# Chunk 0's dense layers woven into the stream that builds the low-rank factors, in a conditioned recurrent kernel

## The chip, the cores and the metric

The kernel runs on one core of one Trainium2 chip. The metric is the device time of one execution in microseconds, the median of several runs.

## What is computed

The reference, cut to what matters (B = 16, T = 512, D = 512, rank 8; `erf` GELU):

```python
c = layernorm(cond) * gamma + beta                  # [16, 512]
h = gelu(c @ W1 + bias1)
w = h @ W2 + bias2                                  # W2 is [512, 16384]
a1, b1, a2, b2 = [t.reshape(B, D, 8) for t in split(w, 4)]
u = einsum('btd,bdr->btr', x, a2)
mid = gelu(x @ down + einsum('btr,blr->btl', u, b2))
v = einsum('blr,btl->btr', b1, mid)
x1 = x + x + mid @ up.T + einsum('bkr,btr->btk', a1, v)
xW = x1 @ Wx + b
h_0 = cond;  h_t = tanh(xW[:, t] + h_{t-1} @ Wh)    # 512 steps, one after the other
y = x1 + h
```

So each batch row has low-rank factors of its own, made from the conditioning vector by one large product with W2 (33.6 MB), and the result of the dense layers drives a recurrence.

## The kernel before

Numbers are split into a high and a low part (`HI`, `LO`) and multiplied in three passes (`PASSES`), so that each product of 128 rows costs three matmuls per 128 of the contraction. The split is two operations: ScalarE rounds the high part (a cast), DVE subtracts it from the number to get the low part. Recurrent weights and states are split in the same way into two 16-bit parts.

Time is cut into NC = 16 chunks of TC = 32 steps; a chunk is 512 columns (16 batches by 32 steps). The work comes in this order:

- **Prologue.** Layer norm of cond on DVE, the product with W1 on TensorE (L795), GELU on ScalarE (L442, L443), transposes of Up (L802) and its split, the split of Down (high half on ScalarE, L426, low half on POOL, L410).
- **The factor stream.** W2 is read in 32 halves of 1 MB through a ring of four buffers of `work` (`load`, L358). For each half n: `w2_high(n)` casts it on ScalarE (L434), `w2_low(n)` subtracts on DVE (L608), TensorE multiplies the high part and then the low part by h, eight matmuls (L835), ScalarE copies the row to `wrow` (L473). Each second half closes a factor tile: TensorE spreads it by eight transposes (L822), DVE sums the parts (L625) and adds the bias (L632, four adds of 64 columns), for half of the tiles TensorE turns it (L810), then ScalarE and DVE split it (L463, L639). There are two pairs of split buffers, `act_s` and `mid_s`. A ring buffer is free when `w2_low` has read it. SP issues everything in its order: the 16 pieces of chunk 0's x (L304) stand between loads, ahead of the last four halves, then Wx and Wh.
- **Chunk 0's dense work.** Slots -23 to 31 of `dense_slot(0, r)` for each engine: transpose x (L661), split it (L491, L669), the rank product U (L850), Mid = x with Down (L861) plus its rank part (L864), GELU and split (L502, L503, L690), the rank product V, Out = Mid with Up, the sum x1 (L694) and its split (L508, L699), XW = x1 with Wx, scaled into `xw` (L513). Each engine walks a list of slots written out ahead (`MID_SLOTS`, `OUT_SLOTS`, `XW_SLOTS`, `XT_AT` and the like). Chunk 0 has nothing beside it but the splits of Wx (L534, L410) and Wh (L537, L770) and the search for Wh's scale.
- **The recurrence.** Step n of chunk c: ScalarE places xW(n) in PSUM (`place`, L481), TensorE multiplies the state by Wh in four quadrants of eight matmuls (L882), DVE sums (L724), ScalarE takes tanh (L529), DVE splits the state (L729, L732), POOL adds the state to x1 (L417). Between steps TensorE does slot t of the dense work of chunk c + 1. Step 0 multiplies by Wh in float32 (L877). In the last chunk three idle matmuls a step take the place of dense work.
- **Store.** x1 plus state is transposed (L707) and stored by SP, 16 DMAs a chunk (L378).

## Time and profile before

| | us |
|---|---|
| median of 3 runs | 1348.98 (1348.88 to 1351.66) |
| the profiled execution | 1356.64 |
| its span, first to last instruction | 1354.9 |
| TensorE busy in the span | 1273.1 (94%) |
| VectorE (DVE) busy | 983.7 (73%) |
| ScalarE (ACT) busy | 702.6 (52%) |
| GpSimd (POOL) busy | 266.6 (20%) |

The profiled execution is 7.7 us above the median; 1.7 us of it lie outside the span. TensorE is busy 90% or more from the sixth of the forty slices on; the first five slices, 170 us, are where it is not. The mean granted TensorE clock is 0.972 of full speed. In the windows below, PEclk is that clock, 1.00 being 2.4 GHz and 0.50 being 1.2 GHz; PE is TensorE's matmuls, PEld its weight loads, SPq the queue that issues DMAs.

### The profile page before, as it was taken

What the parts mean: (1) busy time and instruction counts of PE and PEld (TensorE: products, weight loads), DVE (VectorE), ACT (ScalarE), POOL (GpSimd) and SP (SyncE); (2) the same over time, 40 slices, a digit from 0 to 9 for tenths busy, and PEclk for the clock granted to TensorE, in tenths of its full rate; (3) what the DMA queues carried; (4) which work ended last, traced back from release to release, by engine and by line L of the source; (5) the groups of instructions that cost most, each with busy time, mean ns of one, the idle gap of its engine ahead of it and who ended that gap; (6) DMA issues with size and microseconds to landing.
All of it is one profiled execution on the core that took longest, in us unless ns stands there. A gap on an engine that the chain in (4) does not pass through costs nothing.

```text
span 1354.9 us, 49302 instructions
## 1 busy us (share of the span) xinstructions
PE 1273.1 (94%) x20268; PEld 1019.6 (75%) x20268; DVE 983.7 (73%) x3755; ACT 702.6 (52%) x2499; POOL 266.6 (20%) x525
## 2 busy tenths in 40 slices
PE   6775789999999999999999999999999999999995
PEld 4332478888888888888888888888888888888764
DVE  5665754778787878777777778787878787877564
ACT  5554433555555555555555555555555555555442
POOL 1000010222222222222222222222222222222111
PEclk9788799999999999999999999999999999999998
DMA  8777611113121212121212212111222121202021
GB/s 289 255 246 225 189 26 16 18 18 49 18 49 18 44 24 41 26 42 25 38 30 33 34 28 35 26 31 32 34 33 34 24 43 18 34 3 34 2 34 32
DMA packets 292271, 75.63 MB, mean 56 GB/s; under 512 B 273072, under 2 KB 273088, under 8 KB 292048
## 3 DMA queue, kind: packets, MB, share of 16 engines
q1 hardware_dynamic: 292048, 72.49, 24.0%
q8 instruction: 160, 2.62, 0.9%
q14 instruction: 63, 0.52, 0.2%
HBM read 55.68 MB, written 16.78 MB: 53 GB/s over the span
## 4 chain that ended last, share of the span: by engine, by line
PE 76%; DVE 9%; ACT 7%; issue 3%; DMA 3%; SPq 1%; POOL 0%; DVEq 0%; POOLq 0%; ACTq 0%
PE bulk L861 38%; PE rec L882 28%; PE bulk L850 4%; PE bulk L864 4%; ACT hf L529 3%; DMA work<-in_L_cond_W_dram 2%; DVE act_s L608 2%; PE bulk L835 2%; DVE act_s L699 2%; DVE z L724 2%; ACT rec L481 1%; DVE mid_s L608 1%; SPq L304 1%; DVE work L694 1%; ACT act_s L508 1%
## 5 line engine op out<-in xcount | busy, mean ns | idle before, releaser
L882 PEld LDWEIGHTS rec<-hs,wh_s 128*128 128x128 f16 x16352 | 442.7, 96 | 141.2 <-DVE hs L732 138.1
L529 ACT ACTIVATE hf<-z,scl 128x32 f32<-128x32 f32 x1024 | 273.7, 315 | 499.8 <-DVE z L724 495.5
L882 PE MATMUL rec<-hs,wh_s 128*128 128x32 f16 x16352 | 493.2, 177 | 12.7 <-ACT rec L481 10.4
L417 POOL TENSOR_TENSOR work<-work,hf 128x64 f32<-128x64 f32 x512 | 255.8, 500 | 909.8 <-DVE hs L732 909.8
L724 DVE TENSOR_REDUCE z<-rec 128x32 f32<-128x96 f32 x1024 | 229.8, 255 | 123.2 <-PE rec L882 104.1
L729 DVE TENSOR_SCALAR hs<-hf 128x32 f16<-128x32 f32 x1024 | 181.7, 177 | 106.6 <-ACT hf L529 106.5
L732 DVE SCALAR_TENSOR_TENSOR hs<-hf,hs 128x32 f16<-128x32 f32 x1024 | 197.0, 192 | 35.3
L861 PE MATMUL bulk<-mid_s,up_s 128*128 128x512 f32 x768 | 219.1, 409 | 0.0
L861 PE MATMUL bulk<-act_x,down_s 128*128 128x512 f32 x768 | 218.2, 407 | 0.0
L861 PE MATMUL bulk<-act_s,wx_s 128*128 128x512 f32 x768 | 207.3, 407 | 0.0
L481 ACT ACTIVATE rec<-work 128x32 f32<-128x32 f32 x1024 | 183.9, 209 | 0.0
L861 PEld LDWEIGHTS bulk<-act_s,wx_s 128*128 128x128 f32 x768 | 135.9, 189 | 22.5
L861 PEld LDWEIGHTS bulk<-mid_s,up_s 128*128 128x128 f32 x768 | 132.7, 190 | 17.7
L861 PEld LDWEIGHTS bulk<-act_x,down_s 128*128 128x128 f32 x768 | 132.7, 190 | 17.7
L835 PE MATMUL bulk<-act_s,h_s 128*32 128x512 f32 x128 | 44.0, 480 | 33.8 <-DVE act_s L608 23.1
L513 ACT ACTIVATE work<-bulk,bs,scl 128x512 f32<-128x512 f32 x64 | 48.0, 776 | 23.6 <-PE bulk L861 23.2
L835 PEld LDWEIGHTS bulk<-act_s,h_s 128*32 128x32 f32 x128 | 13.5, 124 | 54.7 <-DVE act_s L608 31.3
L699 DVE TENSOR_TENSOR act_s<-work,act_s 128x512 fp32r<-128x512 f32 x64 | 44.2, 690 | 14.2 <-ACT act_s L508 14.2
L434 ACT CAST act_s<-work 128x2048 fp32r<-128x2048 f32 x16 | 30.5, 1904 | 42.8 <-DVE act_s L608 24.6
L835 PE MATMUL bulk<-mid_s,h_s 128*32 128x512 f32 x128 | 43.8, 485 | 8.1 <-DVE mid_s L608 8.1
L690 DVE TENSOR_TENSOR mid_s<-gel,mid_s 128x512 fp32r<-128x512 f32 x64 | 43.8, 684 | 9.2 <-ACT mid_s L503 9.2
L694 DVE SCALAR_TENSOR_TENSOR work<-work,bulk 128x512 f32<-128x512 f32 x64 | 43.6, 682 | 7.5 <-PE bulk L864 6.2
(114 smaller groups left out, 1027.3 us busy)
## 6 DMA issues: line engine op xcount, KB each, us to landing
work<-in_L_cond_W_dram SPq DMA_DIRECT2D x33, 1024.0 KB, 5.6
work<-in_x_dram SPq DMA_DIRECT2D x256, 64.0 KB, 3.5
out_dram<-work SPq DMA_DIRECT2D x256, 64.0 KB, 2.4
work<-in_L_cond_base_up_dram SPq DMA_DIRECT2D x1, 1024.0 KB, 6.1
work<-in_L_cond_base_down_dram SPq DMA_DIRECT2D x1, 1024.0 KB, 7.7
work<-in_L_cond_Wx_dram SPq DMA_DIRECT2D x1, 1024.0 KB, 4.9
work<-in_L_cond_Wh_dram SPq DMA_DIRECT2D x1, 1024.0 KB, 5.0
bias2T<-in_L_cond_bias_dram SPq DMA_DIRECT2D x4, 16.0 KB, 3.5
```

The costliest lines, as they stand in the source:

```text
L417: nc.gpsimd.tensor_tensor(xs, xs, hf[:, t % 4], ALU.add).then_inc(sum_done, 1)
L481: nc.scalar.activation(R[f][:, :, PARTS, :], xw[:, c % 2].rearrange("p k (b t) -> p k b t", t=TC)[:, f * HT:(f + 1) * HT, :, t], ACT.Copy) ...
L529: nc.scalar.activation(hf[:, t % 4, half], z[:, half], ACT.Tanh, scale=inv).then_inc(tanh_done, 1)
L694: nc.vector.scalar_tensor_tensor(out=x1[n % 3][:, m], in0=x1[n % 3][:, m], scalar=2.0, in1=bulk[:, BANK_OUT[m], :], op0=ALU.mult, op1=ALU. ...
L699: nc.vector.tensor_tensor(act_s[:, LO, m], x1[n % 3][:, m], act_s[:, HI, m].bitcast(F32), ALU.subtract).then_inc(x1lo_done, 1)
L724: nc.vector.tensor_reduce(z[:, f * HT:(f + 1) * HT], R[f].rearrange("p m j b -> p m b j"), AX.X, ALU.add).then_inc(z_done, 1)
L729: nc.vector.tensor_scalar(hs[:, half, 0, :], hf[:, t % 4, half], H_SCALE, None, ALU.mult).then_inc(hi_done, 1)
L732: nc.vector.scalar_tensor_tensor(out=hs[:, half, 1, :], in0=hf[:, t % 4, half], scalar=H_SCALE, in1=hs[:, half, 0, :], op0=ALU.mult, op1=A ...
L835: last = nc.tensor.matmul(bulk[0:2 * B, BANK_ROW + n % 2, :], h_s[:, k].rearrange("p s b -> p (s b)"), w2_s[n % 2][:, part, k, :], start=( ...
L850: last = nc.tensor.matmul(bulk[:, out_bank, g * GC:(g + 1) * GC], fac_s[:, k, g, :], src[:, a, k, g * GC:(g + 1) * GC], start=(k == g == a ...
L861: mm = nc.tensor.matmul(bulk[:, banks[m], :], w_s[:, w, k, m * P:(m + 1) * P], src[:, a, k, :], start=(i in starts), stop=(i in ends), ski ...
L882: last = nc.tensor.matmul(R[fo][:, m, 0:PARTS, :], wh_s[:, q, k, n * P:(n + 1) * P], hs[:, k, :, :], start=(m == k == q == 0), stop=(k == ...
```

## The change

Five things change.

1. Chunk 0's dense work is given a plan of its own (`FIRST`), in pieces fixed by hand: `PE_FILL`, `ACT_FILL` and `DVE_FILL` say behind which half of the stream (0 to 38) each engine does which slots of `dense_slot(0, r)`. Its items are ordered so that the rank parts come late (`first_items`), and TensorE waits once for each factor tile where a piece first needs it. Slots 24 to 31, the product with Wx, come behind the stream, with the first slots of chunk 1. x of chunk 0 is loaded four pieces at a time behind loads 5 to 8 of the ring.
2. Wh is loaded second of all, into a buffer of its own, and its maximum, its scale and its split (high half at half 0, low half at half 1 of the stream) are done ahead. Step 0's product with Wh is done in the prologue, on 16 columns (`first_state`); step 0 is then an add on DVE.
3. A third pair of split buffers, `wx_s`, up to half 17; from half 18 `act_s` and `wx_s` are the two, and `mid_s` serves the dense work. The split of a factor comes one half later on DVE; the bias is added in two operations and not four; `wrow` has memory of its own.
4. PSUM banks are dealt anew, with waits for their release. Chunks 1 to 15 keep their plan but for the slots of x1's low half and of the splits of x. The place of xW for the next step stands ahead of the dense work at a chunk's end too.
5. Small DMAs (norm vectors, bias2) are issued by ScalarE's queue, and half of the last chunk's 16 stores too. Twelve transposes are added on TensorE ahead of its first work.

The diff, cut:

```diff
-BANK_MID = (1, 2, 3, 4)
+BANK_MID = (1, 2, 3, 1)
-BANK_OUT = (5, 1, 2, 3)
-BANK_XW = (4, 5, 1, 2)
+BANK_OUT = (2, 3, 1, 2)
+BANK_XW = (4, 5, 1, 3)
+WARM_MM = 12
+def first_items(kt):
+    items = [(m, k, p) for m in range(kt - 1) for k in range(kt) for p in range(len(PASSES))]
+    items += [(m, g, -1 - w) for m in range(kt - 1) for g in range(GROUPS) for w in (HI, LO)]
+    items += [(kt - 1, k, p) for k in range(kt) for p in range(len(PASSES))]
+    return items + [(kt - 1, g, -1 - w) for g in range(GROUPS) for w in (HI, LO)]
+STREAM = 39
+PE_FILL = {6: (0,), 7: (1,), 8: (2,), 9: (3,), 10: (4,), 11: (5,), 13: (-2,), 21: (6,), 22: (7,), 23: (8,), 27: (12,),
+           28: (13,), 29: (10,), 30: (14,), 31: (15,), 32: (16,), 33: (17, 18), 34: (19,), 35: (20, 21), 36: (22,),
+           37: (23,)}
+ACT_FILL = {3: (-20, -16), 4: (-7, -6), 14: (-2,), 22: (6,), 23: (7,), 24: (8,), 30: (10,), 35: (19,), 36: (20,),
+            37: (21,)}
+DVE_FILL = {2: (-21, -17), 3: (-8, -7), 4: (-6, -5), 5: (-4, -3), 14: (-1,), 15: (0,), 16: (1,), 23: (7,), 25: (8,),
+            26: (9,), 31: (11,), 32: (12,), 33: (13,), 34: (18,), 35: (19,), 36: (20,), 37: (21,), 38: (23,)}
+FIRST_TAIL = 24
+WH_HI_AT, WH_LO_AT, WX_HI_AT = 0, 1, 35
...
-        w2_s = (act_s, mid_s)
+        w2_s = [(act_s, mid_s, wx_s)[n % 3] if n < 18 else (act_s, wx_s)[n % 2] for n in range(HALVES)]
...
+        FIRST = {"u": (-2,) * KT, "v": (10,) * KT,
+                 "mid": stage_plan(first_items(KT), cuts(0, (6, 12, 18, 24, 30, 36, 44, 54, 64))),
+                 "out": stage_plan(first_items(KT), cuts(12, (6, 12, 18, 24, 30, 36, 40, 44, 48, 54, 60, 64))),
+                 "xw": plan(False, FIRST_TAIL, (1,) * 8), "x1lo": (19, 20, 21, FIRST_TAIL)}
...
         def _(sp):
             sp.dma_start(cn[:, 0, :], cond).then_inc(cond_in, 16)
+            sp.dma_start(wh_f, wh.rearrange("(k p) n -> p k n", p=P)).then_inc(wh_in, 16)
             sp.dma_start(w1_f, w1.rearrange("(k p) n -> p k n", p=P)).then_inc(w1_in, 16)
...
+            for e in range(WX_ENTRY + 1):
                 load(e)
+                if e == RING + 1:
+                    sp.wait_ge(hT_mm, 1)
+                if RING < e <= RING + KT:
+                    load_x(0, e - RING - 1)
...
+            store_y(NC - 1, (0, 1))
+            sp.wait_ge(y_out, IN_OUT * NC)
...
         def _(act):
+            for i in range(STREAM):
+                if i + 2 < HALVES:
+                    w2_high(i + 2)
+                if i % 2 and 0 <= i // 2 - 2 <= LAST:
+                    factor_high(i // 2 - 2)
+                if i < HALVES:
+                    row_copy(i)
+                for r in ACT_FILL.get(i, ()):
+                    dense_slot(0, r)
+                if i == WH_HI_AT:
+                    act.wait_ge(scl_done, 1)
+                    nc.scalar.activation(wh_s[:, 0], wh_f, ACT.Identity, scale=w_scale).then_inc(wh_hi, 1)
+                if i == WX_HI_AT:
+                    arrived(act, WX_ENTRY)
+                    nc.scalar.copy(wx_s[:, HI], wx_f).then_inc(w_hi, 1)
...
         def _(dve):
+            for i in range(STREAM):
+                if i < HALVES:
+                    w2_low(i)
+                if i % 2 == 0 and 0 <= i // 2 - 3 <= LAST:
+                    split_factor(i // 2 - 3)
+                if i % 2 == 0 and 0 <= i // 2 - 2 <= LAST:
+                    factor(i // 2 - 2)
...
+                for r in DVE_FILL.get(i, ()):
+                    dense_slot(0, r)
...
         def _(pe):
+            pe.wait_ge(wh_in, 16)
+            pe.wait_ge(h0T_done, 1)
+            first_state(0)
+            first_state(1)
+            pe.wait_ge(ln_chain, 10)
             for k in range(KT):
+                last = nc.tensor.transpose(bulk[:, 0, k * B:(k + 1) * B], cn[:, 1, k * P:(k + 1) * P], ident[0:B, 0:B])
             last.then_inc(cond_tr, 1)
+            first_state(2)
+            first_state(3).then_inc(h0_mm, 1)
...
+                for i in mid[1].get(r, ()):
+                    m, k, p = mid[0][i]
+                    if i in mid[2] and m in (0, 2):
+                        need(pe, xw_done, (n - 1) * KT + 3 + m // 2)
+                    if i in mid[2] and m == KT - 1:
+                        pe.wait_ge(gel_done, n * KT + 1)
+                    if n == 0 and p == -1 and k == 0:
+                        pe.wait_ge(fac_split, KT + m + 1)
...
+            for i in range(STREAM):
+                if i < HALVES:
+                    row(i)
+                if i % 2 and 0 <= i // 2 - 1 <= LAST:
+                    spread(i // 2 - 1)
+                if i % 2 == 0 and 0 <= i // 2 - 2 <= LAST and W2_TILES[i // 2 - 2][0] in (0, 3):
+                    turn(i // 2 - 2)
+                for r in PE_FILL.get(i, ()):
+                    dense_slot(0, r)
```

## Rows read from the trace of the kernel before

**Rows 1.** Timeline of DVE in the stream: start us, us, engine, line, operation, tiles

```profile
28.37 2.29 DVE L608 TENSOR_TENSOR act_s<-work,act_s 128x2048 fp32r<-128x2048 f32 x1 [0.87 <-ACT act_s L434]
...
153.75 2.28 DVE L608 TENSOR_TENSOR act_s<-work,act_s 128x2048 fp32r<-128x2048 f32 x1
...
155.95 0.42 DVE L625 TENSOR_REDUCE fsum<-rec 128x128 f32<-128x256 f32 x1
...
156.40 0.77 DVE L632 TENSOR_TENSOR fac<-fsum,bias2T 128x64 f32<-128x64 f32 x4
157.09 2.28 DVE L608 TENSOR_TENSOR mid_s<-work,mid_s 128x2048 fp32r<-128x2048 f32 x1
```

**Rows 2.** The chain of waits, 186 to 228 us: start us, us, what

```profile
186.62 5.47 PE bulk L861 x24
...
207.19 12.27 PE bulk L861 x48
219.46 1.93 PE bulk L850 x16
...
227.24 0.81 PE rec L882 x32
```

**Rows 3.** Windows by stage: stretch, its length, then each engine's busy us

```profile
core 0: us, PE busy (x) PEld busy (x) DVE busy (x) ACT busy (x) POOL busy (x), PEclk, DMA share, GB/s
26.00:38.00 12.00, 11.36 (x47) 5.12 (x45) 10.32 (x12) 9.51 (x8) 0.00 (x0) 1.00 0.98 353
38.00:50.00 12.00, 6.63 (x24) 2.83 (x23) 6.15 (x9) 7.15 (x7) 0.00 (x0) 0.70 0.71 245
48.00:110.00 62.00, 47.55 (x184) 21.61 (x182) 43.82 (x62) 37.39 (x37) 0.00 (x0) 0.83 0.76 244
...
160.00:222.00 62.00, 55.55 (x255) 45.11 (x253) 33.96 (x61) 20.85 (x33) 4.88 (x1) 0.84 0.22 35
...
228.00:298.60 70.60, 70.17 (x1235) 58.61 (x1234) 51.98 (x222) 38.11 (x150) 16.39 (x32) 1.00 0.10 17
```

**Rows 4.** Timeline around the loads of chunk 0's x; idle time and releaser in brackets

```profile
110.92 13.63 SPq L304 DMA_DIRECT2D work<-in_x_dram  x16
...
132.03 1.90 ACT L434 CAST act_s<-work 128x2048 fp32r<-128x2048 f32 x1 [10.74 <-DMA work<-in_L_cond_W_dram]
```

**Rows 5.** Who waited for whom, 45 to 156 us: us in total, times, longest

```profile
DVE b_s L639 <- ACT b_s L463: 27.7, 8, 10.2
...
DVE a_s L639 <- ACT a_s L463: 15.4, 5, 5.8
```

**Rows 6.** Timeline of the prologue

```profile
9.61 7.01 PE L795 MATMUL bulk<-cT,work 128*128 128x16 f32 x32 [0.99 <-DVE cT L582]
...
14.11 1.90 ACT L426 CAST down_s<-work 128x2048 fp32r<-128x2048 f32 x1 [7.52 <-DMA work<-in_L_cond_base_down_dram]
16.08 4.54 POOL L410 TENSOR_TENSOR down_s<-work,down_s 128x2048 fp32r<-128x2048 f32 x1 [13.71 <-ACT down_s L426]
```

**Rows 7.** The page's costliest groups, one dense operation of DVE: count, busy us, mean ns, idle

```profile
L694 DVE SCALAR_TENSOR_TENSOR work<-work,bulk 128x512 f32<-128x512 f32 x64 | 43.6, 682 | 7.5 <-PE bulk L864 6.2
```

**Rows 8.** Timeline of TensorE in the stream: a spread, a row product, another later

```profile
34.44 1.06 PE L822 MATMUL rec<-ident,wh_s 32*128 32x32 f32 x8
...
35.44 2.04 PE L835 MATMUL bulk<-act_s,h_s 128*32 128x512 f32 x8
...
49.45 3.61 PE L835 MATMUL bulk<-mid_s,h_s 128*32 128x512 f32 x8
```

**Rows 9.** TensorE's waits from 228 to 1275 us: us in total, times, longest

```profile
PE rec L882 <- ACT rec L481: 3.8, 14, 0.3
```

**Rows 10.** The store: SP's issues in the timeline, and what SP waited for last

```profile
1344.63 8.32 SPq L378 DMA_DIRECT2D out_dram<-work  x16
...
SPq L387 <- DMA out_dram<-work: 1.4, 1, 1.4
```

476 lines of the change are left out of this document (228 added, 248 removed).

## The prediction

> **What bounds the kernel now.** I read the stages first (the table of windows), then the order of work on each engine inside the first stages, then who waited for whom, and last the chain of waits at two places. Four stages are to be seen. A prologue; the stream of 32 halves of W2, whose split on DVE ends at 159.37 us [rows 1]; the dense work of chunk 0 alone, until step 1 of the recurrence starts at 227.24 [rows 2]; then the recurrence, 511 steps, with a short store at the end. In the recurrence TensorE is the bound: 70.17 us busy of the 70.60 of a chunk [rows 3]. The first 227 us are different. In the stream TensorE is busy 47.6 of 62 us, DVE 43.8, the DMA engines 76%, the granted clock is 0.83 [rows 3]: nothing is full, the engines wait for each other. The 29 halves from 30.66 to 159.37 took 128.7 us, 4.44 us each [rows 1]. Of these, 10.74 us are one hole at 132 us, ScalarE waiting for a W2 load that SP could only issue after 16 issues of x had held its queue for 13.63 us [rows 4]; without it the pace is 4.07 us. And DVE lost 27.7 + 15.4 us waiting for ScalarE's high half of a factor before its own low half [rows 5]. Then, in the 62 us from 160 to 222, DMA is at 22% and DVE and ScalarE half idle: the dense work of chunk 0 stands alone [rows 3].
>
> **The change, part by part.**
> *Prologue.* TensorE now does 16 matmuls of the first state ahead of the 16 of W1, in the same float32 form; 32 instructions took 7.01 us [rows 6], so up to 7.0 us are added, less the idle time before 9.6 us in which half of them fits. I take W1's product 4.5 us later, ending near 21. The copy of down's high half now stands behind the GELUs of that product, so it starts near 22.5 instead of 14.11; POOL's low half (4.54 us [rows 6]) ends near 29 instead of 20.62. Two ring loads wait on these. W2's first cast waits behind the copy, Up's splits and transposes. New on DVE: Wh's low half in front of half 2, which waits for ScalarE's high half, and that for the row copy. Adding up the queue: low(0) ends at 31.4, low(1) 33.6, Wh's low half 37.3, low(2) near 40, where it was 30.66: **+9.3 us**. Bounds: +6 if first-state work fits the idle time entirely, +12 if the loads released late arrive late as well.
> *Stream.* What goes: DVE's wait for the factor (its split is now one half later, with a third pair of buffers up to half 17), the hole of 10.74 us (x is issued four at a time between loads, at 13.63 / 16 = 0.85 us each, so each load is 3.4 us later once, covered by three loads in flight), two of the four bias adds (0.77 us for four [rows 1]; two wider ones between 0.39 and 0.77, I take 0.53). What comes in: chunk 0's dense work up to the fourth slot of Out. I sum each engine over halves 3 to 31. DVE: 29 x 2.20 (start of low half to the next operation [rows 1]) = 63.8, 14 factors at 0.42 + 0.53 = 13.3, 13 splits at the reduce's 0.42 = 5.5, and 17 dense operations of 128 x 512 (4 transposes, 4 low halves of x, 5 of the rank part, 4 of Mid) at 0.68 [rows 7] = 11.6: 94 us, 3.25 a half. TensorE at full clock: 29 x 8 x 0.228 (5.47 us for 24 [rows 2]) = 52.9, 14 spreads at 1.06 [rows 8] = 14.8, turns some 2.6, Mid 48 x 0.228 + 16 half-width ones = 12.8, the two rank products 2 x 1.93 [rows 2], Out's 24 = 5.5: 92.5 us. DMA: 26 loads of 1.049 MB at 353 GB/s [rows 3] = 77 us, plus what is left of x. Three queues are thus near 3.2 us a half, and they are not full at the same time: halves 2 to 5 carry two dense DVE operations (3.0 + 1.36), halves 6 to 11 and nine later ones six or more dense matmuls (2.04 + 0.53 + 1.4 = 4.0 on TensorE), ten carry nothing. If nothing evened out, the sum of the larger of the two is about 110 us (3.8 a half). The third pair and four ring slots give one to two halves of slack, so I take the middle, **3.5 a half, 101.5 us instead of 128.7: -27.2**. Bounds 94 and 110.
> The clock: TensorE held 1.00 while busy 11.36 of 12 us, and was granted 0.70 in the next 12 us, busy 6.63 [rows 3]; a row product of 8 took 2.04 us at 2.4 GHz and 3.61 at 1.2 [rows 8]. After the change halves 14 to 20 carry no dense matmuls, so I expect some stretches at 1.2 GHz still; at 3.61 + 0.53 a half that is 4.1, no more than 0.6 over my pace, inside the bounds. The Trainium skill (TensorE: Matmul & The Clock Gate, HAM oscillation) says that gaps between bursts throw the clock back and that work without gaps keeps it at full rate. By it the woven pieces would hold 2.4 GHz through the stream; I carry that case as a rival, priced from rows.
> *Behind the stream.* From the end of low(31) to step 1 it was 227.24 - 159.37 = 67.9 us. After: row, copy, spread, factor, turn and ScalarE's split of the last factor take about 6; then its queue has x1's high half and Wx's (1.90), then POOL's low half of Wx, 4.54 [rows 6], which ends some 13 us after low(31). TensorE has Out's last 40 items meanwhile and is done at about 9.5, so XW waits for POOL: the new wait, some 3.5 us, once. XW's 48 matmuls took 12.27, and the 12 rank products of chunk 1 that now stand within them 12/16 of 1.93 = 1.45 [rows 2]; then ScalarE's last tile, the add that replaces step 0's product (3.7 us of TensorE, gone from here), tanh and two splits, 2.2: 13.1 + 13.7 + 2.2 = **29 us, -38.9**. Below: 26 if POOL's part is hidden. Above: XW at half clock after TensorE's idle 3.5 us, 10 more at most.
> *Recurrence.* Sum of matmuls unchanged. Each chunk's first step waited 0.27 us for ScalarE to place xW behind dense work: 14 times, 3.8 us [rows 9]; the place is now ahead of it: **-3.8**, 0 at worst. The banks are dealt anew with four new waits on them; by the slots each is released two slots before it is asked for, taken at nothing. The cover is those two steps (4.4 us); gone, one costs a GELU pair.
> *Store.* 16 issues on SP took 8.32 us, and the last landed 1.4 later [rows 10]: the issues are the bound. Eight go to ScalarE's queue: **-4.1**, 0 if both queues share one issuer. The Trainium skill (DMA: Bandwidth & Descriptors, Issuing engines are not separate DMA queues) says a second issuing engine saves only sequencer time, usually small beside the transfer. By that the sum would be 4 us higher; here the rows show sequencer time as the larger part.
> Sum: 9.3 - 27.2 - 38.9 - 3.8 - 4.1 = -64.7 us. On the profiled execution's 1356.64 that is 1291.9; the median shown is 7.7 below it, so **1284**.
>
> **The rivals.**
> *Full clock, smooth stream* (0.18). If the pieces keep TensorE at 2.4 GHz and the slack evens the halves out, DVE's 94 us set the stream and the tail is 27: 1284 - 7.5 - 2 = 1274.5. For it: the three sums nearly agree. Against: seven halves without pieces.
> *Pieces in series* (0.17). A dense piece waits in TensorE's queue for its factor or GELU with the next row behind it, and that delays row, copy and cast in a ring: the pace stays 4.07, 118 us: 1284 + 16.5 = 1300.5. For it: every engine takes its queue in order, and the old pace came from just such a ring. Against: factors are asked for one half after their split.
> *Nothing is woven* (0.02): if the pieces all stall until the last factors, the dense work of Mid and Out returns behind the stream, some 35 us: 1319.
> *Slower than before* (0.03). The recurrence is 1128 us long, and bank 1 now serves Mid 0, Mid 3, Out 2 and XW 2. If the release by ScalarE or DVE comes late for all four, each stalls TensorE by a GELU pair, 1.2 us, 4.8 a chunk, 72 over 15 chunks: 1356. It decides from 4.3 us a chunk (64.7 / 15). Against: two slots between release and need, and 0.43 us of idle in a chunk today [rows 3].
>
> **How the numbers follow.** The forecast has 0.60, with 1276 to 1295 as its own range. The range for 8 in 10 takes the low rival and the joint lower bounds at 1270, and the series case with part of a half-clock XW at 1303. A measurement of this kernel tells 0.2% (2.7 us) from no change: faster 0.96, same 0.01, slower 0.03.
>
> **What would show it.** Step 1 starts near 170 us; low(2) ends near 40 and low(31) near 142; no wait of DVE on the factor's high half; no hole behind x; POOL's half of Wx just ahead of XW; chunks of 70.3 us; SP's last issues 4 us. I am wrong in the size if low(31) is outside 134 to 150; wrong in kind if the chunks change by over 1 us each or step 1 starts after 190.

## The result and the profile after

| us | before | after |
|---|---|---|
| median | 1350.32 (4 runs, 1348.88 to 1352.69) | 1312.62 (4 runs, 1311.64 to 1315.17) |
| the profiled execution | 1356.64 | 1311.74 |
| its span | 1354.9 | 1310.0 |

The ratio is 0.9722, with a 95% interval of 0.9699 to 0.9745: 38 us faster, where 65 were forecast. 1312.6 lies above the range, which ended at 1303. Stage by stage, from the two profiled executions (low(n) is the low half of W2's half n on DVE; the last add is the last step's add on POOL):

| stage | before | after | measured | forecast |
|---|---|---|---|---|
| prologue, to the end of low(2) | 30.7 | 42.1 | +11.4 | +9.3 |
| stream, low(2) to low(31) | 128.7 | 119.6 | -9.1 | -27.2 |
| behind it, to step 1 | 67.9 | 36.1 | -31.8 | -38.9 |
| recurrence, to the last add | 1116.3 | 1103.1 | -13.1 | -3.8 |
| store | 13.1 | 10.9 | -2.3 | -4.1 |
| sum | | | -44.9 | -64.7 |

Windows of the kernel after, the stream, the stretch behind it and one chunk, which answer to [rows 3], in the same columns:

```profile
42.00:161.70 119.70, 101.11 (x461) 58.24 (x462) 92.69 (x101) 74.64 (x83) 0.00 (x0) 0.89 0.83 257
161.70:197.70 36.00, 32.55 (x159) 25.96 (x158) 20.52 (x35) 13.51 (x24) 4.52 (x1) 0.91 0.21 34
230.00:299.60 69.60, 69.60 (x1239) 58.47 (x1236) 54.55 (x225) 38.14 (x150) 17.92 (x32) 1.00 0.20 33
```

In the stream DVE was busy 92.7 us, where the sum said 94, and TensorE 101.1 with a mean clock of 0.89, where it said 92.5 at full clock. The DMA engines were busy 0.83 of 119.7 us, 99 us, where the sum said 77 and what was left of x: they moved 30.8 MB (257 GB/s) and not 27.3, and 0.83 of their time gave 257 GB/s where [rows 3] had 353 at 0.98. So two of the three sums were low, and the queues did not overlap as evenly as was taken. The last row shows a chunk of 69.60 us in which TensorE never idles, 0.9 less than before.

**The prologue.** Timeline of POOL and DVE in the kernel after (start us, us, engine, line, operation):

```profile
23.74 4.51 POOL L462 TENSOR_TENSOR down_s<-work,down_s 128x2048 fp32r<-128x2048 f32 x1 [21.35 <-ACT down_s L505]
24.77 3.53 DVE L680 TENSOR_SCALAR z0s<-z0s,scl 128x64 f32<-128x64 f32 x1
28.35 2.47 DVE L696 TENSOR_TENSOR up_s<-bulk,up_s 128x512 fp32r<-128x512 f32 x4
```

A scaling of 64 columns took 3.53 us. It started one microsecond after POOL's 4.51 us over Down and ended with it, and low(0), which stands behind it, started at 30.75. The kernel before shows a hold too. Timeline of its DVE:

```profile
18.79 3.98 DVE L608 TENSOR_TENSOR act_s<-work,act_s 128x2048 fp32r<-128x2048 f32 x1 [7.62 <-ACT act_s L434]
```

This is low(0), 3.98 us where the other low halves take 2.29, beside the POOL instruction of [rows 6], which ended at 20.62.

**The stream.** Timelines of DVE and TensorE in the kernel after, at three places where a half took much longer than 3.5 us:

```profile
47.74 0.71 DVE L728 STREAM_TRANSPOSE work<-work 128x512 f32<-128x512 f32 x1 [2.27 <-DMA work<-in_x_dram]
53.64 0.71 DVE L728 STREAM_TRANSPOSE work<-work 128x512 f32<-128x512 f32 x1 [5.18 <-DMA work<-in_x_dram]
...
97.80 0.68 DVE L741 TENSOR_TENSOR both<-both,bulk 64x512 f32<-64x512 f32 x1 [4.05 <-ACT both L549]
...
128.06 1.67 PE L928 MATMUL bulk<-act_x,down_s 128*128 128x512 f32 x6 [2.07 <-ACT mid_s L556]
```

Half 3 to 4 took 11.0 us: DVE stood in front of chunk 0's last two tiles of x, which had not landed, with half 4's subtraction queued behind. Half 14 to 15 took 9.0: DVE asked for the rank product while ScalarE's copy of it was not yet made. At 128 us TensorE asked for Mid's GELU before ScalarE had made it (half 23 to 24 took 5.8). A fourth stretch, low(9) to low(13), ran at 3.82 a half with TensorE busy 15.30 of 15.30 us, as the prediction's 4.0 had it.

**Behind the stream.** Timeline of the four engines before XW, in the kernel after:

```profile
173.59 1.91 ACT L583 CAST wx_s<-work 128x2048 fp32r<-128x2048 f32 x1
175.58 4.52 POOL L462 TENSOR_TENSOR wx_s<-work,wx_s 128x2048 fp32r<-128x2048 f32 x1 [147.33 <-ACT wx_s L583]
176.05 5.19 DVE L766 TENSOR_TENSOR act_s<-work,act_s 128x512 fp32r<-128x512 f32 x2 [0.71 <-ACT act_s L561]
180.15 12.46 PE L928 MATMUL bulk<-act_s,wx_s 128*128 128x512 f32 x42 [3.45 <-POOL wx_s L462]
```

The new wait stands where it was forecast, 3.45 us where "some 3.5" was said. That its size fits is in part luck, since both of its ends came some 5 us late: TensorE was done with Out 15.0 us after low(31) and not 9.5, POOL 18.4 and not 13. XW's 42 matmuls took 12.46 us, where 42 take 9.8 at full clock (measured below): the granted clock was half from 179.0 to 185.8, and 5.7 us of that lie in XW. DVE's two subtractions, 0.69 each elsewhere, took 5.19 together; the first was held until POOL had ended.

**The recurrence.** Timeline of TensorE over three steps of one chunk, slots 18 to 20, in the kernel before:

```profile
545.47 0.96 PE L882 MATMUL rec<-hs,wh_s 128*128 128x32 f16 x32
...
547.80 0.96 PE L882 MATMUL rec<-hs,wh_s 128*128 128x32 f16 x32
...
550.07 0.96 PE L882 MATMUL rec<-hs,wh_s 128*128 128x32 f16 x32
```

and the same slots in the kernel after:

```profile
512.39 0.96 PE L944 MATMUL rec<-hs,wh_s 128*128 128x32 f16 x32
...
514.44 0.97 PE L944 MATMUL rec<-hs,wh_s 128*128 128x32 f16 x32
...
516.51 0.97 PE L944 MATMUL rec<-hs,wh_s 128*128 128x32 f16 x32
```

Steps of 2.33 and 2.27 us became 2.05 and 2.07, with the same matmuls in between: 0.28 and 0.20 gained. The list of waits of before names neither; TensorE was busy in both, as its rows have it.

**The store.** Issues and SP's last wait in the kernel after:

```profile
1302.00 4.21 SPq L335 DMA_DIRECT2D out_dram<-work  x8
1302.00 4.35 ACTq L335 DMA_DIRECT2D out_dram<-work  x8
...
SPq L128 <- DMA out_dram<-work: 3.4, 1, 3.4
```

The issues went from 8.32 to 4.35 us [rows 10], and the wait behind them from 1.4 to 3.4.

### The profile page after: what moved, and what is told of

It reads as the page before. It is cut to its first block, busy times and chain, and to the rows that moved or that the text cites. A ratio compares the mean times of both kernels' runs of the same rounds, so it can differ in the third digit from the quotient of the medians.

```text
span 1310.0 us, 49303 instructions
## 1 busy us (share of the span) xinstructions
PE 1258.5 (96%) x20280; PEld 1021.1 (78%) x20280; DVE 990.0 (76%) x3723; ACT 701.6 (54%) x2497; POOL 288.9 (22%) x525
## 4 chain that ended last, share of the span: by engine, by line
PE 85%; ACT 2%; DVE 2%; issue 0%; POOL 0%; DVEq 0%; POOLq 0%; ACTq 0%
PE bulk L928 43%; PE rec L944 31%; PE bulk L917 5%; PE bulk L931 5%; ACT hf L593 1%; PE bulk L907 1%; DVE z L804 1%; ACT rec L534 1%; PE rec L894 0%; POOL wx_s L462 0%; DVE work L774 0%; DVE wx_s L689 0%; ACT wx_s L583 0%; DVE hs L812 0%; DVE hs L809 0%
## 5 line engine op out<-in xcount | busy, mean ns | idle before, releaser
L469 POOL TENSOR_TENSOR work<-work,hf 128x64 f32<-128x64 f32 x512 | 278.4, 544 | 842.7 <-DVE hs L812 842.7
L812 DVE SCALAR_TENSOR_TENSOR hs<-hf,hs 128x32 f16<-128x32 f32 x1024 | 197.2, 193 | 35.3
L728 DVE STREAM_TRANSPOSE work<-work 128x512 f32<-128x512 f32 x64 | 44.8, 703 | 7.5 <-DMA work<-in_x_dram 7.5
L766 DVE TENSOR_TENSOR act_s<-work,act_s 128x512 fp32r<-128x512 f32 x64 | 47.6, 745 | 1.9 <-ACT act_s L561 1.9
L931 PE MATMUL bulk<-rank_s,b_s 128*128 128x256 f32 x256 | 45.6, 292 | 0.0
L931 PE MATMUL bulk<-rank_s,a_s 128*128 128x256 f32 x256 | 45.6, 292 | 0.0
L757 DVE TENSOR_TENSOR mid_s<-gel,mid_s 128x512 fp32r<-128x512 f32 x64 | 43.8, 684 | 2.2 <-ACT mid_s L556 2.2
L761 DVE SCALAR_TENSOR_TENSOR work<-work,bulk 128x512 f32<-128x512 f32 x64 | 43.6, 681 | 2.3 <-PE bulk L931 0.9
L774 DVE STREAM_TRANSPOSE work<-work 128x512 f32<-128x512 f32 x64 | 44.7, 703 | 0.7 <-POOL work L469 0.5
```

The lines of the kernel that those rows point to most:

```text
L469: nc.gpsimd.tensor_tensor(xs, xs, hf[:, t % 4], ALU.add).then_inc(sum_done, 1)
L766: nc.vector.tensor_tensor(act_s[:, LO, m], x1[n % 3][:, m], act_s[:, HI, m].bitcast(F32), ALU.subtract).then_inc(x1lo_done, 1)
L812: nc.vector.scalar_tensor_tensor(out=hs[:, half, 1, :], in0=hf[:, t % 4, half], scalar=H_SCALE, in1=hs[:, half, 0, :], op0=ALU.mult, op1=A ...
L931: mm = nc.tensor.matmul(bulk[:, banks[m], k * GC:(k + 1) * GC], rank_f[:, -1 - p, k, m * P:(m + 1) * P], rank_s[:, k * GC:(k + 1) * GC], s ...
```

## The experiments

All edits are against the kernel after, unless said otherwise. "Tail" is from the end of low(31) to the first add on POOL, which comes beside step 1 (36.3 in after). Stages are those of one profiled execution each. In the variants, e9 apart, the stream began 0.5 to 1.6 us later than in after's own profile, and in the kernels whose stream is that of after it took 119.6 to 122.6 us: a stage is read to 1 or 2 us, no closer. The tail varies too where nothing in it was edited: 36.2 to 36.4 in most, but 35.3 in e14 and 34.5 in e5. Medians come from four or five timings, on several chips; the five variants whose median lies within 0.6 us of after's (e2, e4, e8, e9, e12) have ratios from 0.9706 to 0.9721, a spread of 2 us, so a median is not read closer than that either. Line numbers of variants are shifted by a few.

| run | median us | ratio to before, 95% | low(2) ends | stream | tail |
|---|---|---|---|---|---|
| after | 1312.6 | 0.9722 (0.9699 to 0.9745) | 42.1 | 119.6 | 36.3 |
| e1, no pieces in the stream | 1319.8 | 0.9762 (0.9744 to 0.978) | 43.5 | 99.1 | 61.6 |
| e2, x turned later | 1312.9 | 0.9706 (0.9691 to 0.9722) | 43.4 | 119.5 | 36.2 |
| e3, two pairs | 1315.9 | 0.9731 (0.9716 to 0.9747) | 42.7 | 122.3 | 36.3 |
| e4, Wx cast early | 1312.4 | 0.9706 (0.969 to 0.9722) | 43.4 | 121.2 | 34.3 |
| e5, rank piece later | 1310.9 | 0.9704 (0.9683 to 0.9724) | 43.5 | 117.1 | 34.5 |
| e6, old place | 1320.4 | 0.9768 (0.9747 to 0.979) | 43.7 | 122.0 | 36.3 |
| e7, old slots of x1's low half | 1322.8 | 0.9787 (0.9765 to 0.9809) | 43.5 | 122.6 | 36.2 |
| e8, z0 scaled later | 1313.2 | 0.9721 (0.9702 to 0.9741) | 43.4 | 119.6 | 36.2 |
| e9, both scaled behind Up | 1312.9 | 0.9716 (0.9703 to 0.973) | 41.0 | 122.5 | 36.2 |
| e10, x loaded earlier | 1309.6 | 0.9684 (0.967 to 0.9697) | 42.9 | 115.4 | 36.2 |
| e11, e4 + e5 + e9 + e10 | 1303.5 | 0.9642 (0.9629 to 0.9656) | 43.3 | 112.1 | 34.3 |
| e12, idle matmuls ahead of XW | 1312.8 | 0.9714 (0.97 to 0.9727) | 42.8 | 122.1 | 34.6 |
| e13, Wx's low half on DVE | 1309.3 | 0.9697 (0.9678 to 0.9715) | 43.5 | 120.5 | 30.7 |
| e14, GELU pieces later | 1308.5 | 0.9698 (0.968 to 0.9717) | 43.6 | 114.5 | 35.3 |
| e15, e11 + e13 | 1298.1 | 0.962 (0.9605 to 0.9636) | 43.0 | 110.0 | 30.7 |
| e16, e15 + e14 | 1296.3 | 0.9599 (0.9581 to 0.9617) | 43.5 | 107.5 | 30.7 |
| e17, the kernel before | 1350.7 | 1.0001 (0.9986 to 1.0015) | 30.5 | 126.0 | 64.7 |
| e18, one store queue | 1316.4 | 0.9758 (0.9745 to 0.977) | 42.6 | 122.2 | 36.3 |

### The whole weaving undone, and the third pair

e1 puts every piece of dense work behind the stream.

```diff
-PE_FILL = {6: (0,), 7: (1,), 8: (2,), ...
+PE_FILL = {38: (-2, 0, 1, 2, ..., 23)}
+ACT_FILL = {38: (-20, -16, -7, ..., 21)}
+DVE_FILL = {38: (-21, -17, -8, ..., 23)}
```

> The changed kernel with all of chunk 0's pieces put behind the stream (one after the other at place 38), everything else kept. Pieces theory: the stream was slowed by pieces that stood in an engine's queue waiting for a late input; without them the 29 halves from low(2) to low(31) take about 100 us (3.4 a half) instead of 119.6, and step 1 then starts some 60 us behind low(31). Loads theory: the halves are late because W2 and x come late; then the 29 halves still take 115 us or more. Time in both cases 1325 to 1345 us.

Windows of e1, the stream:

```profile
43.50:142.60 99.10, 81.60 (x356) 39.14 (x356) 82.21 (x86) 68.67 (x71) 0.00 (x0) 0.90 0.91 300
```

Without pieces a half takes 3.42 us, with the DMA engines at 91%. So the pieces cost 20.5 us in the stream and save 25.3 behind it, 4.8 net in these two profiles, and weaving by itself is worth 7 us in the median (5 by the ratios); the expectation's 1325 to 1345 us for the whole was missed. ScalarE waited 23.4 us for loads of W2 in this stream, and 91% is the highest share of the DMA engines in any stream here: that the loads set the pace of 3.42 is argued from these two numbers. The other 31 us of the change's gain come from what else it does; the recurrence and the store are 15 of them (below). Of the rest, the loads of x that no longer stop those of W2, the factor asked for later, and Wh and step 0's product out of the tail, this run shows only the sum.

e3 takes the third pair of split buffers away.

```diff
-        w2_s = [(act_s, mid_s, wx_s)[n % 3] if n < 18 else (act_s, wx_s)[n % 2] for n in range(HALVES)]
+        w2_s = [(act_s, mid_s)[n % 2] if n < 18 else (act_s, wx_s)[n % 2] for n in range(HALVES)]
```

> The third pair of split buffers is taken away (halves 0 to 17 use two pairs, as the kernel before did). If the third pair gave slack as I forecast, halves 6 to 17 get slower by 0.3 us each or more and the time rises by 4 to 10 us; if TensorE's sum of work sets their pace, it rises by under 2 us.

It is worth about 3 us (1315.9 against 1312.4 to 1312.9 on the same chip), between the two theories: some slack, but not the 4 us or more that were expected of it. The stage does not show it, since a stream of 122.3 us is within what untouched ones took.

### The stream's holes, one at a time

e2 turns and splits the late tiles of x one or two halves later.

```diff
-ACT_FILL = {3: (-20, -16), 4: (-7, -6), ...
-DVE_FILL = {2: (-21, -17), 3: (-8, -7), 4: (-6, -5), 5: (-4, -3), ...
+ACT_FILL = {3: (-20, -16), 5: (-7, -6), ...
+DVE_FILL = {2: (-21, -17), 4: (-6, -5), 5: (-8, -7), 6: (-4, -3), ...
```

> The transposes of x's last two parts move on DVE from behind half 3 to behind half 5, and the casts and low halves that follow them one or two halves. Pieces theory: DVE's 7.5 us of waiting for x (2.27 and 5.18) stood ahead of low(4) and goes almost whole; low(4) starts near 46 instead of 54.27 and the time falls by 4 to 7 us. Loads theory: half 6's load landed only at 52.7, so low(6) stays near 60 and the time falls by under 2 us.

DVE's hole went: low(4) started at 46.8 where it was 54.3. Then ScalarE waited 3.44 and 2.90 us for W2's loads, and low(7) started at 64.2 (65.5 in after). The rest went on TensorE, where the first pieces of Mid now met half clock (67.6 to 74.4 us): a row product took 3.42 us and six dense matmuls 2.93, low(10) to low(11) took 8.0 us for 5.4, and low(11) started at 80.0 (79.5 in after). So DVE's order alone did not make the hole; the loads of W2 stand among 16 issues of x on SP, which e10 tries.

e10 loads x two tiles at a time, and earlier.

```diff
-                if e == RING + 1:
+                if e == RING - 1:
                     sp.wait_ge(hT_mm, 1)
-                if RING < e <= RING + KT:
-                    load_x(0, e - RING - 1)
+                    load_x(0, 0)
+                    load_x(0, 1)
+                if RING <= e <= RING + 1:
+                    load_x(0, e - RING + 2)
```

> Chunk 0's x is issued earlier: two of its four parts ahead of the load that waits for Up's transposes, the third behind it, the fourth behind the next. Loads theory (x's 128-byte pieces and W2's loads share SP and the DMA engines in the window where halves 3 to 7 are due, and the idle window at 20 to 30 us costs nothing): the wait of DVE for x (7.5 us) and ScalarE's waits for halves 5 and 6 go, low(7) starts near 59 instead of 65.5, and the time falls by 4 to 7 us. Rival: as when the transposes were moved, TensorE's sum of work gives it back by half 11, and the time falls by under 2 us.

DVE's wait for x is gone from its list, the stream is 4.2 us shorter and the median 3.0 lower, or 3.7 without one of its five timings, 3627 us, an outlier that the ratio leaves out; 4 to 7 were expected.

e5 gives DVE the rank piece one half later.

```diff
-DVE_FILL = {..., 14: (-1,), 15: (0,), 16: (1,), ...
+DVE_FILL = {..., 15: (-1,), 16: (0,), 17: (1,), ...
```

> The three DVE pieces of the rank sum U (slots -1, 0, 1) move one half later, so that DVE takes low(15) before it waits for ScalarE's copy of U. Pieces theory: the hole between low(14) and low(15), 9.0 us with 4.05 us of DVE waiting, shrinks to about 4.5 us and the time falls by 3 to 5 us. Sum theory (TensorE and its clock set the pace there): under 1.5 us.

The half of 9.0 us became 4.3, yet the stream is only 2.5 shorter and the median 1.7, between the two theories and at the edge of what the timings tell: from low(15) to low(21) it took 23.25 us for 19.67 and so gave 3.6 of the 4.7 back.

e14 moves the last two pieces of Mid (slots 7 and 8) by one half, on TensorE and on ScalarE.

```diff
-PE_FILL = {..., 21: (6,), 22: (7,), 23: (8,), 27: (12,),
-ACT_FILL = {..., 22: (6,), 23: (7,), 24: (8,), ...
+PE_FILL = {..., 21: (6,), 23: (7,), 24: (8,), 27: (12,),
+ACT_FILL = {..., 22: (6,), 24: (7,), 25: (8,), ...
```

> Edit: after, with pieces 7 and 8 of the dense work on TensorE, and on ScalarE, one half later each (23, 24 and 24, 25 instead of 22, 23 and 23, 24). Theory A: the halves 23 to 28 at 4 to 5.8 us come from TensorE asking for ScalarE's GELU (wait of 2.07 us) before it is done, with the next row behind it. Then that wait is gone, and the stream is 1 to 3 us shorter: 116.6 to 118.6 against 119.6; time 1310 to 1312. Theory B: those halves are bound by TensorE's sum of rows, spread, turn and pieces, or by what comes in late behind them; then the wait goes or moves, and the stream stays at 119 to 121, time 1312 to 1314.

Timeline of TensorE in e14, the place of the 2.07 us:

```profile
130.95 1.55 PE L928 MATMUL bulk<-act_x,down_s 128*128 128x512 f32 x6
```

No wait stands ahead of the Mid piece. The stream fell by 5.1 us, more than expected. From half 21 to 27 it gained 2.8 us (22.0 for 24.8), and from there to half 31 another 2.5, where after had a stretch of half clock (145 to 152 us) and e14 had none. That the one follows from the other is argued, not shown.

### Behind the stream: POOL over Wx

e4 casts Wx's high half behind half 32, so that POOL starts earlier.

```diff
-WH_HI_AT, WH_LO_AT, WX_HI_AT = 0, 1, 35
+WH_HI_AT, WH_LO_AT, WX_HI_AT = 0, 1, 32
```

> ScalarE's cast of Wx moves from place 35 to place 32 of the stream, ahead of its wait for x1's first tile. Tail theory (XW waits for POOL's low half of Wx, 3.45 us, and TensorE's clock falls because of that wait): POOL ends before TensorE is done with Out, the wait goes, XW's 42 matmuls take near 9.7 us instead of 12.46, and the time falls by 4 to 7 us. Rival: only the wait itself goes, 3.5 us, the clock falls all the same; or POOL's half now collides with DVE's queue and under 2 us are left.

Timeline of POOL and DVE in e4:

```profile
170.45 4.72 POOL L462 TENSOR_TENSOR wx_s<-work,wx_s 128x2048 fp32r<-128x2048 f32 x1 [140.92 <-ACT wx_s L583]
170.80 4.66 DVE L750 CAST rank_s<-rank 64x512 fp32r<-64x512 f32 x1
```

The rank cast, 0.42 us in after, took 4.66 and ended 0.3 us behind POOL. TensorE no longer waits for Wx but for Out's rank part, 1.5 us, and XW's 42 matmuls took 9.78 us at full clock. Tail -2.0, median the same: of the expectation, the rival held.

e12 puts 13 matmuls whose result nobody reads ahead of XW.

```diff
+            for k in range(13):
+                nc.tensor.matmul(bulk[:, BANK_IDLE, :], down_s[:, HI, 0, 0:P], mid_s[:, HI, k % KT, :],
+                                 start=True, stop=True)
```

> Thirteen idle matmuls of 512 columns on TensorE between Out and XW, in the 3.45 us in which it waits for POOL. Clock theory (the wait lets the clock fall to 1.2 GHz in the middle of XW, 6.8 us of it): XW's 42 matmuls take near 9.7 us instead of 12.46, and the time falls by 2 to 3 us. If the clock does not depend on that wait, the time is the same within 1 us.

XW's 42 matmuls ran at full clock, 18 in 4.39 us and 24 in 5.78, with two waits of half a microsecond. The tail fell by 1.7 us. The median did not move, with a stream of 122.1 us in its profile. But this does not show that the idle matmuls kept the clock. Timeline of TensorE in e5, which leaves this stretch as it is in after:

```profile
179.15 4.38 PE L928 MATMUL bulk<-act_s,wx_s 128*128 128x512 f32 x18 [3.46 <-POOL wx_s L462]
184.01 5.75 PE L928 MATMUL bulk<-act_s,wx_s 128*128 128x512 f32 x24 [0.48 <-DVE act_s L766]
```

The same wait, no idle matmuls, and full clock all the same. In this one stretch the two profiles, after's and e5's, differ by the clock alone: it is worth 1.8 us of tail (36.3 and 34.5). Whether idle matmuls help would take several profiles of e12.

e13 casts Wx as e4 does, and gives its low half to DVE.

```diff
-            for n, (src, dst) in enumerate(((down_f, down_s), (wx_f, wx_s))):
+            for n, (src, dst) in enumerate(((down_f, down_s),)):
...
+                if i == 33:
+                    dve.wait_ge(w_hi, 2)
+                    nc.vector.tensor_tensor(wx_s[:, LO], wx_f, wx_s[:, HI].bitcast(F32), ALU.subtract).then_inc(w_split, 1)
```

> Edit: after, with Wx's high half cast by ScalarE behind half 32 instead of 35, and its low half taken by DVE behind half 33 instead of by POOL; POOL then does nothing between the factor stream and the recurrence. Theory A (port hold): in the kernel after, POOL's 4.52 us over Wx held DVE's two factor splits 5.19 us and TensorE waited 3.45 us for it at half clock afterwards. Then without POOL: the first matmul of XW no later than 16.5 us after low(31) ends (18.5 in after), no wait of TensorE on wx_s, XW's 42 matmuls in about 9.8 us (12.46 in after), stage from low(31) to step 1's first add 32 to 33 us (36.3 in after). DVE pays 2.3 us for the low half inside the stream, so the stream is 0 to 2 us longer. Time 1308 to 1312. Theory B (the tail is bound by ScalarE's and TensorE's own work, POOL's part lies beside it): tail 35.5 or more, time 1312 to 1315.

Windows of e13 from the end of low(31) to the first add, and TensorE's only wait from 160 to 195 us:

```profile
164.00:194.70 30.70, 30.25 (x169) 24.21 (x168) 18.90 (x37) 13.50 (x24) 0.00 (x0) 1.00 0.28 45
...
PE rec L885 <- DVE fac L714: 0.5, 1, 0.5
```

and its timeline of DVE and TensorE:

```profile
171.40 2.29 DVE L794 TENSOR_TENSOR wx_s<-work,wx_s 128x2048 fp32r<-128x2048 f32 x1
...
179.53 9.81 PE L931 MATMUL bulk<-act_s,wx_s 128*128 128x512 f32 x42
```

TensorE is busy 30.25 of 30.70 us at full clock. The tail lost 5.6 us and stands at 30.7, near the 29 of the forecast and below the 32 to 33 expected. So the cast's late place and POOL's instruction over Wx made 5.6 of the 7.1 us by which that term was missed. With the cast early and POOL still at work the tail was 34.3 (e4); with all as in after but the full clock it was 34.5 (e5), so 3.8 us are left for the late cast, POOL's hold on DVE and TensorE's wait. The low half on DVE with the cast in its old place was not tried, so the two parts of the edit are not told apart.

### The prologue's scalings

e8 moves only the scaling of z0 into the stream; e9 moves both scalings behind Up's splits.

```diff
-            nc.vector.tensor_scalar(z0s[:], z0s[:], fwd, None, ALU.mult)
...
+                if i == 10:
+                    nc.vector.tensor_scalar(z0s[:], z0s[:], fwd, None, ALU.mult)
```

> DVE's scaling of the first state's product, 64 columns, which took 3.53 us beside POOL's low half of Down, moves to behind half 10. If DVE was held by POOL through the port that they share, the operation takes about 0.2 us there, low(0) starts near 29 instead of 30.75 and the time falls by 1 to 3 us. If it was held by something of its own, it takes over 3 us again.

> Both small DVE scalings that follow Wh's scale (64 and 4 columns) move behind Up's four splits, which read PSUM and one SBUF operand. Port theory: whichever small scaling came first beside POOL's low half of Down was held until POOL ended (3.53 us for 64 columns, 3.50 us for 4 columns once the first was moved); behind Up's splits, near POOL's end, they take about 0.3 us together, Up's first two splits run beside POOL, low(0) starts 1 to 2 us earlier than in the kernels of the last calls (32.1) and the time falls by 0 to 2 us. Rival: POOL holds Up's splits too, and nothing changes.

Timeline of DVE in e8:

```profile
26.27 3.50 DVE L680 TENSOR_SCALAR bs<-vT,scl 128x4 f32<-128x4 f32 x1
```

and in e9:

```profile
25.95 1.29 DVE L694 TENSOR_TENSOR up_s<-bulk,up_s 128x512 fp32r<-128x512 f32 x2
...
29.33 0.24 DVE L777 TENSOR_SCALAR z0s<-z0s,scl 128x64 f32<-128x64 f32 x1
```

The hold passed on, so e8 saved none of the 1 to 3 us that were expected. Whichever scaling comes beside POOL is held, even one of 4 columns; a subtraction with one operand in PSUM (`bulk`) is not, and runs beside POOL in its usual time. With e9 low(0) started 2.5 us earlier than in e8 (29.6 for 32.1; 30.75 in after), and lost it again at half 4, where x was awaited: no gain in the median.

### The recurrence

e6 puts the place of the next chunk's first step behind the dense work again, e7 puts the four low halves of x1 back to their old slots.

```diff
-                    for f in range(2) if n + 1 < T else ():
+                    for f in range(2) if n + 1 < T and t + 1 < TC else ():
...
+                    for f in range(2) if t == TC - 1 and c + 1 < NC else ():
+                        place(n + 1, f)
```

> ScalarE's placing of xW for the first step of a chunk goes back behind the dense work, as before; nothing else. The chunks were 70.5 us before and 69.6 after. If the order of the place gave half of that, chunks come to about 70.05 us, the last step of a chunk 0.45 us longer, and the time rises by 6 to 7 us. If it gave only the 0.27 us that the trace called a wait, it rises by 4 us.

```diff
-X1LO_SLOT = (18, 20, 22, 23)
+X1LO_SLOT = (17, 18, 20, 22)
```

> The slots of x1's low half in chunks 1 to 15 go back to those of before (17, 18, 20, 22). If these slots made the two late steps at slots 18 and 19 (0.48 us a chunk), chunks come to about 70.05 us and the time rises by 7 us; if not, it stays within 1 us and the two late steps were made by something else (the splits of x, the banks).

A chunk takes 70.02 us in e6 and 70.08 in e7, 69.60 in after and 70.50 in before: 0.42 and 0.48, together the 0.90 that a chunk gained. Fifteen times 0.90 is 13.5 us; the last chunk, which has no dense work, took 0.35 more in after, which leaves the 13.1 of the table. The medians rose by more than fifteen chunks give, 7.8 for 6.3 us and 10.2 for 7.2; their profiled streams were 2.4 and 3.0 us longer than after's, within what untouched ones take. TensorE's waits in e6 from 230 to 1245 us:

```profile
PE rec L946 <- ACT rec L534: 3.8, 14, 0.3
```

After has none up to 1230 us. This is the place's part, and a list of waits shows it, though at 0.27 us for 0.42; that of x1's slots no list shows, since it sits in the pace of steps in which TensorE has work queued.

### Together, the baseline, and the store

e11 joins e4, e5, e9 and e10; e15 adds e13's edit to it; e16 adds e14's. No other edit is in them. e15 is 5.4 us below e11, e16 1.9 below e15. e11 and e16 came as expected; e15 did better than its better theory (1301 to 1303), with a tail of 30.7 for 32 to 33 and a stream of 110.0 for 112 to 114.

> x early, the rank sum one half later, Wx's cast at place 32 and the small scalings behind Up's splits, all at once. If each hole is its own, the gains add up to 8 to 12 us (1301 to 1305 us). If the stream is held by TensorE's sum of work at 84% busy, under 5 us.

> Edit: the combination that ran before (x loaded earlier, the rank piece later, scalings of z0 and bs behind Up's splits, Wx's cast behind half 32) with Wx's low half on DVE behind half 33 instead of on POOL. In that combination rank_s was still held by POOL's 4.7 us. Theory A: with POOL out of it the stage from low(31) to the first add is 32 to 33 us (34.3), the stream 112 to 114 (112.1): time 1301 to 1303, less only if the 2.3 us of DVE fit its idle time. Theory B: no shorter tail, time 1303 to 1306.

> Edit: the kernel above with pieces 7 and 8 one half later too. Theory A: 1 to 3 us less than the kernel above. Theory B (a hole's gain is taken by the next queue that is late): within 1 us of it.

Windows of e16, the stream and the tail, and the longest of TensorE's waits in the stream:

```profile
43.40:151.00 107.60, 99.08 (x461) 58.10 (x462) 92.45 (x101) 75.61 (x83) 0.00 (x0) 0.91 0.88 285
151.00:181.60 30.60, 30.14 (x168) 24.11 (x166) 18.88 (x37) 13.42 (x24) 0.00 (x0) 1.00 0.26 42
...
PE bulk L912 <- DVE wx_s L689: 12.2, 5, 4.7
```

e16 is the fastest kernel here, 54 us below before and 16.4 below after. A hole's worth depends on what else is mended. The GELU pieces gave 5.1 us of stream alone and 2.5 in company. In the other direction, the scalings gave nothing alone, and with x loaded early low(4) no longer takes it back; that this is a part of e11's 9.1 us was not tried by itself. The stream now takes 3.70 us a half, with TensorE, DVE and the DMA engines at 92%, 86% and 88%: near the 3.5 of the forecast, but only after four repairs, and near the 3.42 that it takes without pieces (e1).

e17 profiles the kernel before a second time.

> Edit: none; the kernel before, profiled a second time. Its first profiled execution was 1356.64 us, 6 to 8 above every median of its timings, and the prediction carried that difference over as if it lay in parts that the change leaves alone. Theory A: it lies in the stream, in when loads arrive (the stage that the change rewrites): then the second profile is within 3 us of the median 1350 and its stream from low(2) to low(31) is 122 to 126 us instead of 128.7, with prologue, tail and chunks as they were within 1 us; the true gain in medians is then 6 us less than in these profiles. Theory B: it lies outside the stream (recurrence or ends): the stream is again 128 to 129.5 us. Theory C: a profiled execution of this kernel is always longer: 1355 or more again.

The second profile is 1350.80 us, 5.8 less than the first: 2.7 of it in the stream (126.0) and 3.2 in the tail (64.7), with chunks of 70.5 in both. Theory A held for the stream and missed the tail. Timelines of ScalarE, the load of half 6 in before and in e17:

```profile
40.43 1.90 ACT L434 CAST act_s<-work 128x2048 fp32r<-128x2048 f32 x1 [3.64 <-DMA work<-in_L_cond_W_dram]
37.56 1.91 ACT L434 CAST act_s<-work 128x2048 fp32r<-128x2048 f32 x1 [0.90 <-DMA work<-in_L_cond_W_dram]
```

That load came 2.9 us earlier, and low(5) to low(6) took 5.9 us for 8.3: most of the stream's 2.7. Windows of e17 at the first two stretches of [rows 3]:

```profile
26.00:38.00 12.00, 11.37 (x46) 5.29 (x45) 10.78 (x12) 9.75 (x9) 0.00 (x0) 0.85 1.03 367
38.00:50.00 12.00, 7.97 (x32) 3.36 (x31) 7.42 (x9) 7.92 (x8) 0.00 (x0) 0.86 0.84 287
```

Same kernel, same instructions: the granted clock is 0.85 and 0.86 where it was 1.00 and 0.70, and the DMA engines' share in the second window 0.84 where it was 0.71. Behind the stream the clock was full from 155.9 us on, where in before it was half until 172.4 with breaks: U's first 12 matmuls took 1.75 us for 2.51, and that is where the tail's 3.2 us are. When the half clock falls and when a load lands differ between executions, and with them the length of both stages that the change rewrites.

e18 gives all 16 stores back to SP.

```diff
-            store_y(NC - 1, (0, 1))
+            store_y(NC - 1, range(P // SQ))
...
-                    move_y(act, NC - 1, k, i)
+                    pass
```

> Edit: after, with all 16 stores of the last chunk issued by SP again, none by ScalarE. Theory A (the issues were the bound before, the transfer of short pieces now): SP's issues take 8.3 us again, the wait behind them falls from 3.4 to 1.4 us, the stretch from the last add to the end grows by 2.3 us from 9.1 to 11.4: time 1314 to 1316. Theory B (the prediction's: a second queue is worth 4.1 us): 4 us longer, 1316 to 1318. Theory C (both queues share one issuer, the second is worth nothing and the 2.3 us came from elsewhere): 1312 to 1313.5, end 9 to 9.5 us.

Timeline of SP in e18 and its last wait:

```profile
1305.18 8.32 SPq L335 DMA_DIRECT2D out_dram<-work  x16
...
SPq L128 <- DMA out_dram<-work: 1.4, 1, 1.4
```

From the last add to the end of the span it is 11.3 us for 9.1: the second queue is worth 2.2 us, as theory A has it. The median rose by 3.8 to 1316.4, more than this stage and just inside theory B's range, but the stream of its profile is 2.6 us longer than after's, within what an untouched stream varies.

## Why the prediction was wrong, point by point

By the prediction's own signs it was wrong in the size, since low(31) ended at 161.7 us and not within 134 to 150, and by the start of step 1, at 197.7 and so after 190, wrong in kind as well. The chunks changed by 0.90 us each, just under its limit of 1.

**The prologue** (+9.3, came +11.4). The added matmuls and the late Down came as summed; low(0) ended 1.6 us late (33.0 for 31.4), and Wh's low half, which waited 2.31 us for ScalarE, added another microsecond. Left out was that DVE would be held beside POOL. The row was at hand: [rows 6] gave POOL's 4.54 us, low(0) beside it took 3.98 us for 2.29, and the change moved that work beside DVE's chain. The Trainium skill (SBUF — State Buffer, Who interferes with whom) says that GpSimd and DVE share one pair of ports, held by whoever starts first for its whole instruction, that copies, casts and tensor_scalar may ask for it, and any DVE operation with both inputs in SBUF. The traces agree in each case: the scalings (3.53, 3.50), the cast (4.66) and a subtraction within SBUF (two in 5.19, of which the second took 0.68) were held; the subtraction from PSUM was not.

**The stream** (-27.2, came -9.1) is the step that failed: "the third pair and four ring slots give one to two halves of slack, so I take the middle, 3.5 a half". The three sums were right for DVE, 9% low for TensorE, whose mean clock was 0.89, and further off for the DMA engines: 77 us and what was left of x, against 99 us busy in after, 90 in e1 (0.91 of 99.1) and 95 in e16. These three streams moved 29.7 to 30.8 MB at 310 to 330 GB/s of busy time, where the sum had 27.3 MB at 353: 3.1 to 3.4 us a half and not 2.7. And "if nothing evened out" was taken as the sum of the larger of two queues, 110 us, and that is no upper bound: it holds only if no engine stands in front of something that is not there. 119.6 came. In three places one did: x not landed behind its own issues on SP, the rank product not copied, the GELU not made. A fourth stretch, where TensorE was full, was the only one that the sum had. With the three mended, and the edits of prologue and tail, e16's stream took 107.5 us, inside 94 to 110. The cover for loads held up by 3.4 us each, "three loads in flight", was not there at half 4. The rival "pieces in series" gave 118 us and 1300.5, and its mechanism, a piece in the queue with the next row behind it, is what the GELU and the rank piece showed. That case deserved more than 0.17; its "against" spoke of factors only, where x, the rank product and the GELU were late.

**The clock.** The mean granted clock in the stream was 0.89 with the pieces and 0.90 without them (e1): weaving changed it hardly at all, and the rival at full clock fell. Its price shows at XW: 42 matmuls took 12.46 us with 5.7 of them at half clock, and 9.81 at full clock (e13). Eleven kernels, after among them, waited 3.45 to 3.47 us for POOL ahead of XW: nine were at half clock for 6.8 us around it, e14 for 3.4, e5 not at all. Of those without that wait, e1, e13, e15 and e16 kept 2.4 GHz there; e4 and e11, which waited 1.5 us for the rank part instead, were at half clock for 3.4 us ahead of XW. The Trainium skill's rule (TensorE: Matmul & The Clock Gate, HAM oscillation), that gaps between bursts throw the clock back and gapless work keeps it up, fits all of these but e5: the same gap does not cost the clock every time.

**Behind the stream** (29, came 36.1). The wait for POOL was forecast in place, and in size partly by luck, both of its ends being 5 us late. Missed were three things. Out ended 15 us after low(31) and not 9.5, and ScalarE's cast of Wx stood behind the split of the last factor, for whose turn it waited 4.30 us, since TensorE had that turn behind pieces of Out. POOL would hold DVE (the same port). And XW after the idle time runs partly at half clock, which stood only in the upper bound ("10 more at most"), and cost 1.8 us (after against e5). e13 takes POOL and the half clock away, moves the cast as well, and leaves 30.7.

**The recurrence** (-3.8, came -13.1). The mechanism was right and its size 6.3 us for 3.8: the wait on the place, 0.27 by the list [rows 9], cost 0.42 in the chunk's length. The slots of x1's low half, worth 7.2, were named in the change and not costed at all. The four new waits on the banks cost nothing, as taken; the rival that was slower has no sign in the trace.

**The store** (-4.1, came -2.3). Issues halved as said. Then the transfer is late: 16 stores of 64 KB, 1.05 MB, from the first issue at 1302.0 to 4.2 + 3.4 us later, 138 GB/s where the stream of W2 runs at 353 [rows 3]. The Trainium skill's rule (DMA: Bandwidth & Descriptors, Issuing engines are not separate DMA queues), that a second issuing engine saves only sequencer time, usually small beside the transfer, came out in between: 3.97 us of issue time went and 2.0 us of waiting for the transfer came.

**From the profile to the median.** Of the 28.6 us between 1284 and 1312.6, 19.8 are the stages and 8.8 the last step: 7.7 us were subtracted because the profiled execution stood that much above its median, as if this lay in parts that the change leaves alone. e17 shows 5.8 of it in the two stages that it rewrites, and after's own profile lies 0.9 below its median. Against the second profile of before the true gains are 6.4 us in the stream and 28.4 behind it.

## What to carry to other kernels

Busy sums of the engines bound a woven schedule from below only: for each piece ask, on each engine's queue, what is not there yet when it comes up and what is queued behind it, and let the consumer's slot follow the producer's by one more step. Cost the small reorderings inside a loop first: 0.48 us a chunk was worth as much as the whole weaving of the dense work. Sum the DMA engines with all that they move in the stretch, at the rate of a whole stretch and not of its best window. Before moving a POOL instruction, look at what DVE runs beside it, and take the length of a stage in which the clock changes, and what an edit does to that clock, from several profiles, not one.
